# Unit 0's query tiles moved between the wide value tiles, and head pair 1 made from seven half products

## The chip, the core and the metric

The kernel runs on one core of one Trainium2 chip. The time is the device time of one execution in microseconds; several executions are taken, and their median counts. The engines are TensorE (PE, matmuls into PSUM), VectorE (DVE), ScalarE (ACT), GpSimd (POOL) and SyncE (SP, which issues most DMAs). Each runs its own list of instructions in order and waits on semaphores.

## The reference

Four layers on x of 16 x 64 rows of width 512, each added to x. The change lies in the first, an attention over a context of the same shape. Cut to that layer:

```
d, h, kv_h, g = 128, 32, 8, 4
q = rope((layernorm(x) @ Wq).reshape(b, t, 32, 128))
k = rope((ctx @ Wk).reshape(b, t, 8, 128))
v = (ctx @ Wv).reshape(b, t, 8, 128)
logits = 30 * tanh(q . k * 0.0884 / 30), masked
attn = softmax(logits) . v
x = x + attn.reshape(b, t, 4096) @ Wo
```

Behind it come a small mixture of low-rank experts, a second attention with 16 heads of 96, and a dense layer with 16 low-rank updates.

## The kernel before

All matmuls of width 512 are in float32 made from two parts: every operand is split into a high part (a copy by ACT) and a low part (the difference, by DVE or POOL), and a product takes three matmuls (high-high, high-low, low-high). A query or key tile is 128 x 512: one head's 128 columns for half of the 1024 rows, four chunks of the depth by three matmuls, twelve matmuls.

The first attention is worked through in 16 units. Unit u takes the four heads of one key head (u // 2) for one half of the rows (u % 2). Its stages: queries in four tiles, rope on them, `b0` (queries times keys, a burst of 16 short matmuls in banks 2 and 3), tanh and exp on ACT, the mask on POOL (L1271), `sum0` on DVE (transposes, a sum, a reciprocal, L1716 to L1729), a trip of the reciprocals through memory and back (`sum0_out` on SP), `norm0` (L1733), `d0` (weights times values), and `e0` (times Wo, four tiles of twelve matmuls, added to x in `e0_add`, L1547).

The queries of key head 0 (units 0 and 1) are tiles `q0(u, n)`, each with its rope. Those of the later heads come from "pairs": pair u gives two heads for all rows, and is worked in while unit u runs; it serves unit u + 2 or u + 3. A pair can be made in two ways. Plain: four tiles `pp(u, t)`, 12 matmuls each, 48 in all. By half products: seven products `p(u, k)` of 6 matmuls, 42 in all, after the manner of fast matrix multiplication by sums of blocks. That takes sums of blocks of x (made once, `xt`, split by `xt_split` into Th on ACT and Tl on DVE or POOL, L1658 and L1227), sums of blocks of the pair's weights (four 128x256 pieces on POOL, `add_weights`, L1190 to L1195, split by `pair` in one 1024 wide piece, L1220), three copies of partial results (`snap`, ACT) and three additions (`cmb`, DVE, L1618). Which pairs are plain is set by one constant, `PLAIN = 2`: pairs 0 and 1.

A rope is three DVE instructions (L1695, L1696, L1698), which read the PSUM tile and so free its bank, and one addition on POOL (L1250). A weight split is one copy on ACT (L1328) and one difference on POOL (L1213), from a ring of four staging buffers that SP fills three splits ahead.

The order is written by hand in `plan()`: a list of steps, and every engine's program goes through the same list and takes its part of each step. So a step's place in the list sets its place in the queue of each engine that has a part in it. `stage` gives a tile a PSUM bank from a ring and the step. Ahead of unit 0 stand the key tiles `k0`, the value tiles `v0`, and eight wide value tiles `vq(n)` of twelve matmuls, each copied out by ACT and sent to memory. vq, the pair of weights WS0 and the halves Th and Tl share places in memory, so that split wp(1, n) and xt_split wait for the last vq tile. The lines below have the numbers that the profile shows.

## Time and profile before

| what | value |
|---|---|
| runs | 816.91, 817.16, 817.37 us |
| median | 817.16 us |
| the profiled execution | 817.04 us, its span 815.2 us |
| busy in the span | PE 808.3, DVE 605.9, POOL 440.0, ACT 393.9 us |
| PE idle in 150 to 200 us | 1.92 us |
| PE idle in 250 to 300 us | 0 us |

The span runs from the first to the last instruction that the profiler saw. Times in the rows are microseconds from the span's start. A matmul's shown length includes its way through the array, so that the next may start before it ends; the distance of the starts is what it costs. A long length of a DVE or POOL instruction can hold a wait inside it.

### The profile page before, as it was taken

The numbers are of one execution on the slowest core, as the hardware profiler recorded it, in microseconds if no ns is written. First come the engines' busy times: TensorE is split into PE (matmuls) and PEld (weight loads), VectorE is DVE, ScalarE is ACT, GpSimd is POOL, SyncE is SP. The second block draws the span as 40 slices with busy tenths as digits, with TensorE's granted clock in tenths as the row PEclk, the third lists the DMA queues.
The fourth block names the chain that finished last, engine by engine and source line by source line (L and its number), as shares of the span: only waits on it lengthen the run. The fifth ranks groups of instructions, "written<-read, shape, count | busy, mean of one in ns | idle before, by whom it ended". The sixth has DMA issues, their size and how long they took to land.

```text
span 815.2 us, 12015 instructions
## 1 busy us (share of the span) xinstructions
PE 808.3 (99%) x4278; PEld 670.1 (82%) x4278; DVE 605.9 (74%) x1143; ACT 393.9 (48%) x960; POOL 440.0 (54%) x342
## 2 busy tenths in 40 slices
PE   9999999999999999999999999999999999999998
PEld 8898877777787777887777788899888888888887
DVE  6887579998888978888798566464466657678894
ACT  4233313334234343233433342667787777787762
POOL 4797389866767786676874520112232531365442
PEclk9999999999999999999999999999999999999999
DMA  9468402322232232322214730001110210300002
GB/s 345 157 185 339 143 14 69 100 66 72 86 117 67 77 104 77 119 78 66 77 54 126 256 105 1 27 27 52 27 27 27 66 27 14 129 15 1 1 1 104
DMA packets 34476, 70.16 MB, mean 86 GB/s; under 512 B 5360, under 2 KB 8688, under 8 KB 33776
## 3 DMA queue, kind: packets, MB, share of 16 engines
q1 hardware_dynamic: 31872, 64.54, 25.3%
q10 hardware_dynamic: 2544, 4.85, 1.7%
q8 instruction: 34, 0.56, 0.3%
q14 instruction: 26, 0.21, 0.1%
HBM read 57.70 MB, written 11.67 MB: 85 GB/s over the span
## 4 chain that ended last, share of the span: by engine, by line
PE 74%; POOL 2%; issue 1%; DVE 0%; ACT 0%; DMA 0%; ACTq 0%; POOLq 0%
PE PB L1855 14%; PE PB L1857 14%; PE PB L1856 14%; PE PB L1902 11%; PE PB L2117 8%; PE PB L2132 4%; PE PB L1862 3%; PE PB L2044 3%; PE PB L2027 2%; PE PB L2065 1%; PE PB L2079 0%; POOL W L1213 0%; DMA stage<-in_wo 0%; POOL WVl L1213 0%; POOL WSl L1213 0%
## 5 line engine op out<-in xcount | busy, mean ns | idle before, releaser
L1250 POOL TENSOR_TENSOR qb<-qb,arena 128x512 f32<-128x512 f32 x76 | 105.6, 1395 | 109.5 <-DVE arena L1698 109.5
L1328 ACT ACTIVATE Oh<-PB 96x128 fp32r<-96x128 f32 (+2 forms) x236 | 79.2, 359 | 44.6 <-PE PB L2044 25.5
L1547 DVE TENSOR_TENSOR xs<-xs,PB 128x512 f32<-128x512 f32 x111 | 73.2, 682 | 36.9 <-PE PB L1857 28.0
L1213 POOL TENSOR_TENSOR WVl<-stage,WVh 128x512 fp32r<-128x512 f32 (+1 forms) x25 | 33.6, 1359 | 70.8 <-ACT WVh L1328 64.3
L1855 PE MATMUL PB<-WVh,Oh 128*128 128x512 f32 x158 | 62.2, 394 | 0.7 <-DVE arena L1698 0.4
L1856 PE MATMUL PB<-WVl,Oh 128*128 128x512 f32 x158 | 61.5, 389 | 0.0
L1857 PE MATMUL PB<-WVh,Ol 128*128 128x512 f32 x158 | 61.5, 389 | 0.0
L1328 ACT ACTIVATE WSh<-wsum 128x1024 fp32r<-128x1024 f32 x12 | 12.7, 1061 | 91.6 <-POOL wsum L1195 91.6
L1855 PE MATMUL PB<-W,Oh 128*128 128x512 f32 x142 | 55.6, 391 | 0.8 <-POOL W L1213 0.8
L1213 POOL TENSOR_TENSOR WQl<-stage,WQh 128x512 fp32r<-128x512 f32 x17 | 22.7, 1343 | 61.0 <-ACT WQh L1328 52.2
L1857 PE MATMUL PB<-W,Ol 128*128 128x512 f32 x142 | 55.3, 389 | 0.0
L1856 PE MATMUL PB<-W,Oh 128*128 128x512 f32 x142 | 55.3, 389 | 0.0
L1695 DVE TENSOR_TENSOR qb<-PB,ropeq 128x512 f32<-128x512 f32 x64 | 44.0, 688 | 15.1 <-PE PB L1977 6.4
L1824 DVE TENSOR_TENSOR Ol<-PB,Oh 64x128 fp32r<-64x128 f32 (+2 forms) x172 | 49.2, 286 | 7.0 <-ACT Oh L1328 3.5
L1741 DVE TENSOR_TENSOR Ol<-PB,Oh 128x512 fp32r<-128x512 f32 x64 | 39.7, 682 | 18.7 <-ACT Oh L1328 18.6
L1510 ACT ACTIVATE Eb<-PB,sm 128x128 f32<-128x128 f32 x128 | 45.2, 366 | 8.9 <-DVE sm L1803 8.5
L1696 DVE TENSOR_TENSOR arena<-PB,ropeq 64x512 f32<-64x512 f32 x64 | 44.3, 693 | 0.8
L1803 DVE TENSOR_REDUCE sm<-PB 128x4 f32<-128x512 f32 x32 | 21.9, 685 | 30.7 <-PE PB L2132 30.7
L1698 DVE TENSOR_TENSOR arena<-PB,ropeq 64x512 f32<-64x512 f32 x64 | 43.7, 683 | 0.8
L2117 PE MATMUL PB<-xTh,WQh 128*128 128x512 f32 x96 | 39.8, 414 | 0.0
L2117 PE MATMUL PB<-xTh,WQl 128*128 128x512 f32 x96 | 37.7, 392 | 0.0
L2117 PE MATMUL PB<-xTl,WQh 128*128 128x512 f32 x96 | 37.6, 392 | 0.0
(343 smaller groups left out, 2457.2 us busy)
## 6 DMA issues: line engine op xcount, KB each, us to landing
stage<-in_wq SPq DMA_DIRECT2D x44, 256.0 KB, 2.8
stage<-in_wo SPq DMA_DIRECT2D x44, 256.0 KB, 2.8
arena<-recs SPq DMA_DIRECT2D x32, 256.0 KB, 3.9
stage<-in_wk SPq DMA_DIRECT2D x12, 256.0 KB, 3.8
keys<-qb SPq DMA_DIRECT2D x12, 256.0 KB, 3.2
arena<-keys SPq DMA_DIRECT2D x6, 512.0 KB, 3.3
xs<-in_x SPq DMA_DIRECT2D x8, 256.0 KB, 7.0
xf<-in_xT SPq DMA_DIRECT2D x4, 512.0 KB, 10.8
```

The lines of the kernel that those rows point to most:

```text
L1213: e.tensor_tensor(lo, src, hi.bitcast(f32), ALU.subtract).then_inc(s_wlo)
L1250: e.tensor_tensor(dst, dst, tmp, ALU.add).then_inc(s_radd)
L1328: return e.activation(dst, src, ACT.Copy)
L1510: last = e.activation(Eb[:, e2, cols], PS[:, cols], ACT.Exp, bias=mx[:, bb:bb + 1], accum_out=rs[:, bb:bb + 1])
L1547: e.tensor_tensor(xs[:, i, :], xs[:, i, :], PB[b][:, :], ALU.add).then_inc(free[b])
L1696: e.tensor_tensor(tmp[0:64], src[64:128], table[64:128, 1:2, :].broadcast_to([64, 8, 64]), ALU.mult)
L1824: last = e.tensor_tensor(dl, PA[bank_of("d1", t, bank)][d0:d0 + rows, h], dh.bitcast(f32), ALU.subtract)
L1855: e.matmul(dst, Ah, Bh, start=(k == 0), stop=False)
L1856: e.matmul(dst, Ah, Bl, start=False, stop=False)
L1857: return e.matmul(dst, Al, Bh, start=False, stop=(k == n - 1))
L1902: last = e.matmul(PB[b][:, :], W[:, w], X[:, c, :], start=fresh and c == n == 0, stop=(c == 1 and n == 2), skip_group_check=not fresh)
L2117: last = e.matmul(PB[b][:, :], W[:, m, r], H[:, c, cols], start=(n % 12 == 0), stop=(n % 12 == 11))
```

## The change

`PLAIN` becomes 1, so pair 1 is made by half products, and its products are spread over the list, with the plain tiles pp(0, 2) and pp(0, 3) between them. The tiles q0(0, 0) to q0(0, 3) stand between vq(3) and vq(7) instead of behind them. The four xt_splits come in the order (0,0), (1,0), (0,1), (1,1), of which only (1,0) has its low part on POOL, where two had it. The four splits of wo0 for units 0 and 1 stand in units 0 and 1 one by one. The steps of unit 2 get the order of the later units.

```
@@ -8,7 +8,7 @@
 NU = 16
 N1 = 32
 LO, HI = range(0, 4), range(4, 8)
-PLAIN = 2
+PLAIN = 1
 D0_BANKS = (0, 1, 4, 6)
 SLOTS = (4, 5, 6, 7, 0, 1, 2, 3)
 PARTS = {1: (0, 256), 2: (256, 512), 4: (512, 768), 5: (768, 1024), 6: (1024, 1280), 7: (1280, 1536), 3: (1536, 1792)}
@@ -303,16 +303,17 @@
     for n in range(3, 8):
         vq(n)
         spill_v(n - 1)
+        if n < 7:
+            q0(0, n - 3)
+        if n == 5:
+            step("sums", 1)
     spill_v(7)
-    q0(0, 0)
-    step("xt_split", 0, 0)
-    for n in range(1, 4):
-        q0(0, n)
     ring.remove(2)
     pair(1)
-    for n in (1, 0):
-        q0(1, n)
-    step("xt_split", 0, 1)
+    step("xt_split", 0, 0)
+    split("wo0", 0)
+    q0(1, 0)
+    step("xt_split", 1, 0)
 
     def products(u, *ks):
         for k in ks:
@@ -340,36 +341,42 @@
 
         if u == 0:
             burst(0)
+            q0(1, 1)
+            split("wo0", 1)
+            step("xt_split", 0, 1)
             q0(1, 3)
-            q0(1, 2)
-            q0p(0, 0, 5)
             step("sum0", 0)
             step("sum0_out", 0)
-            step("xt_split", 1, 0)
-            step("sums", 2)
-            q0p(0, 1, 7)
+            split("wo0", 2)
+            q0(1, 2)
+            step("xt_split", 1, 1)
+            q0p(0, 0, 6)
+            q0p(0, 1, 4)
+            norm0(0)
             continue
         if u == 1:
+            products(1, 1, 2)
             burst(1)
-            step("xt_split", 1, 1)
-            q0p(0, 2, 0)
-            q0p(0, 3, 4)
+            products(1, 5)
+            rope_p(1, 0)
+            q0p(0, 2, 1)
+            split("wo0", 3)
+            products(1, 6, 3)
+            rope_p(1, 1)
+            products(1, 7)
+            rope_p(1, 2)
+            q0p(0, 3, 3)
             for n in range(2):
                 split("wp", 2, n)
-            q0p(1, 0, 6)
-            norm0(0)
+            products(1, 4)
+            rope_p(1, 3)
+            step("sum0", 1)
+            step("sum0_out", 1)
             step("k_in", 2)
-            q0p(1, 1, 1)
             step("pair", 2)
-            q0p(1, 2, 2)
-            q0p(1, 3, 3)
-            for n in range(4):
-                split("wo0", n)
             continue
         quad = u + 2 < NU
         paired = u < NU - 3
-        if u == 2:
-            products(2, 1, 2)
         if u == NU - 2:
             step("ctx_in", 0)
         burst(u)
@@ -377,27 +384,19 @@
             step("k_in", (u + 3) // 2)
         if u in (5, 9):
             step("v_in", (u - 5) // 4)
-        if u == 2:
-            step("sum0", 1)
-            step("sum0_out", 1)
-        if u >= 4:
-            norm0(u - 1)
+        norm0(u - 1)
         if u == NU - 2:
             for m in range(3):
                 split("wk1", m, 0)
             for c in range(2):
                 split("wv1", c)
         if quad:
-            if u >= 3:
-                products(u, 1, 2)
+            products(u, 1, 2)
             products(u, 5)
             rope_p(u, 0)
-        if u == 3:
-            norm0(2)
-        if u >= 3:
-            step("sum0", u)
-            if u < NU - 1:
-                step("sum0_out", u)
+        step("sum0", u)
+        if u < NU - 1:
+            step("sum0_out", u)
         outputs(0)
         if quad:
             products(u, 6, 3)
@@ -413,19 +412,13 @@
         if u == NU - 2:
             step("ctx_in", 1)
         added(0, 1)
-        if u == 2:
-            norm0(1)
-            added(2)
         if quad:
             products(u, 4)
             rope_p(u, 3)
         if paired:
             step("pair", u + 1)
-        if u == 2:
-            step("sum0", u)
-            step("sum0_out", u)
         outputs(3)
-        added(*((3,) if u == 2 else (2, 3)))
+        added(2, 3)
         if u % 2:
             for n in range(4):
                 split("wo0", 2 * u - 2 + n)
@@ -1042,7 +1035,7 @@
                 return (("k0", 6, 1), ("vq", 7))[k[0]] if k[0] < 2 else ("p", k[0] - 2, 4) if k[0] >= 2 + PLAIN else ("pp", k[0] - 2, 3)
             if kind == "wo0":
                 h = k[0] - 4
-                return ("e0", h // 4 * 2 + 1, 3) if h >= 0 else ("q0", 1, 3)
+                return ("e0", h // 4 * 2 + 1, 3) if h >= 0 else (("vq", 7), ("q0", 1, 0), ("q0", 1, 1), ("q0", 1, 2))[k[0]]
             if kind == "wk1":
                 return {(0, 0): ("p", 13, 4), (1, 0): ("p", 13, 4), (2, 0): ("p", 13, 4), (0, 1): ("k1", 0, 0, 1),
                         (1, 1): ("k1", 0, 1, 1), (2, 1): ("k1", 1, 1, 1)}[k]
@@ -1220,10 +1213,9 @@
                     e.tensor_tensor(lo[:, 768:1792], wsum[:, :], hi[:, 768:1792].bitcast(f32), ALU.subtract).then_inc(s_wslo)
                 elif kind == "xt_split":
                     kk, hf = k
-                    if (kk + hf) % 2:
-                        n = 2 * kk + hf
+                    if (kk, hf) == (1, 0):
                         hi, lo, src = (H[:, 2 * kk:2 * kk + 2, 512 * hf:512 * hf + 512] for H in (Th, Tl, xf))
-                        pool.wait_ge(s_thi, n + 1)
+                        pool.wait_ge(s_thi, 2)
                         e.tensor_tensor(lo, src, hi.bitcast(f32), ALU.subtract).then_inc(s_tlo[1])
                 elif kind == "many":
                     pool.wait_ge(s_tab, 16)
@@ -1441,8 +1433,8 @@
                         if u:
                             act.wait_ge(*done("e0", u - 1, 3))
                         else:
-                            act.wait_ge(s_tlo[0], 2)
-                            act.wait_ge(s_tlo[1], 2)
+                            act.wait_ge(s_tlo[0], 3)
+                            act.wait_ge(s_tlo[1], 1)
                         move(dh, src).then_inc(s_ohi)
                 elif kind == "ffn_xT":
                     i, = k
@@ -1652,9 +1644,9 @@
                     e.tensor_tensor(b[1, 1], b[1, 1], b[0, 1], ALU.subtract).then_inc(s_xt)
                 elif kind == "xt_split":
                     kk, hf = k
-                    if (kk + hf) % 2 == 0:
+                    if (kk, hf) != (1, 0):
                         hi, lo, src = (H[:, 2 * kk:2 * kk + 2, 512 * hf:512 * hf + 512] for H in (Th, Tl, xf))
-                        dve.wait_ge(s_thi, 2 * kk + hf + 1)
+                        dve.wait_ge(s_thi, 2 * hf + kk + 1)
                         e.tensor_tensor(lo, src, hi.bitcast(f32), ALU.subtract).then_inc(s_tlo[0])
                 elif kind == "rope":
                     n = ropes[tuple(k)]
@@ -1886,7 +1878,7 @@
                     pe.wait_ge(*(lo_ready("wp", u, t // 4) if t in (1, 2, 4) else (s_wslo, u - PLAIN + 1)))
                     pe.wait_ge(*x_ready(1))
                     if t in (4, 5, 6, 7):
-                        pe.wait_ge(s_tlo[t in (6, 7)], 1 + (t in (4, 7)))
+                        pe.wait_ge(s_tlo[t == 7], {5: 1, 6: 2, 4: 3, 7: 1}[t])
                     if t == 6:
                         pe.wait_ge(s_snap, 3 * (u - PLAIN) + 1)
                     elif t == 3:
```

Where instructions stand on the engines shows in three places. On DVE, behind the reciprocal of unit 0's sum0: the names are tiles, PB0 to PB7 the PSUM banks, Tl the low part of x's block sums. Before, the bank of the plain tile pp(0,1) is roped there, then xt_split(1,1), then the plain tiles of unit 1's stretch:

```order
L1729 RECIPROCAL rec<-rec 64x32
L1695 TENSOR_TENSOR qb<-PB7,ropeq 128x8x64
L1696 TENSOR_TENSOR arena<-PB7,ropeq 64x512
L1698 TENSOR_TENSOR arena<-PB7,ropeq 64x512
L1658 TENSOR_TENSOR Tl<-xf,Th 128x2x512
L1695 TENSOR_TENSOR qb<-PB0,ropeq 128x8x64
L1696 TENSOR_TENSOR arena<-PB0,ropeq 64x512
L1698 TENSOR_TENSOR arena<-PB0,ropeq 64x512
L1695 TENSOR_TENSOR qb<-PB4,ropeq 128x8x64
```

Now q0(1,2) is roped there, then xt_split(1,1), and then the two first plain tiles of pair 0, and then comes norm0(0):

```order
L1721 RECIPROCAL rec<-rec 64x32
L1687 TENSOR_TENSOR qb<-PB1,ropeq 128x8x64
L1688 TENSOR_TENSOR arena<-PB1,ropeq 64x512
L1690 TENSOR_TENSOR arena<-PB1,ropeq 64x512
L1650 TENSOR_TENSOR Tl<-xf,Th 128x2x512
L1687 TENSOR_TENSOR qb<-PB6,ropeq 128x8x64
L1688 TENSOR_TENSOR arena<-PB6,ropeq 64x512
L1690 TENSOR_TENSOR arena<-PB6,ropeq 64x512
L1687 TENSOR_TENSOR qb<-PB4,ropeq 128x8x64
L1688 TENSOR_TENSOR arena<-PB4,ropeq 64x512
L1690 TENSOR_TENSOR arena<-PB4,ropeq 64x512
L1725 TENSOR_TENSOR Eb<-Eb,arena 128x1024
```

What moved: sum0(0) stands two ropes earlier than before, so that both plain tiles come behind it and behind the xt_split; the first cmb of pair 1 follows norm0(0). On POOL, in the stretch of unit 1, before, from the rope addition that follows the wsum pieces of pair 2:

```order
L1250 TENSOR_TENSOR qb<-qb,arena 128x8x64
L1271 TENSOR_TENSOR pTb<-pTb,keep 128x1024
L1250 TENSOR_TENSOR qb<-qb,arena 128x8x64 x2
L1213 TENSOR_TENSOR WSl<-stage,WSh 128x512
L1213 TENSOR_TENSOR WSl<-stage,WSh 128x256
L1250 TENSOR_TENSOR qb<-qb,arena 128x8x64 x2
L1220 TENSOR_TENSOR WSl<-wsum,WSh 128x1024
L1250 TENSOR_TENSOR qb<-qb,arena 128x8x64 x2
L1213 TENSOR_TENSOR WVl<-stage,WVh 128x512 x2
L1213 TENSOR_TENSOR W<-stage,W 128x512 x2
```

Now the wsum pieces of pair 2 stand behind the rope additions of unit 1, directly ahead of the split of wp(2,0) (WSl, 512 wide):

```order
L1242 TENSOR_TENSOR qb<-qb,arena 128x8x64 x2
L1206 TENSOR_TENSOR W<-stage,W 128x512
L1242 TENSOR_TENSOR qb<-qb,arena 128x8x64 x3
L1183 TENSOR_TENSOR wsum<-stage 128x256
L1184 TENSOR_TENSOR wsum<-stage 128x256
L1186 TENSOR_TENSOR wsum<-wsum,stage 128x256
L1188 TENSOR_TENSOR wsum<-stage,wsum 128x256
L1206 TENSOR_TENSOR WSl<-stage,WSh 128x512
L1206 TENSOR_TENSOR WSl<-stage,WSh 128x256
L1242 TENSOR_TENSOR qb<-qb,arena 128x8x64
```

What moved: the splits of pair 2 and its sums stand behind all rope additions but one, and the split of wo0 stands between these. On PE, ahead of the burst b0 of unit 2, before, the last two matmuls of p(2,2) and then d0(0):

```order
L1902 MATMUL PB7<-xTl,WSh1 128x512
L1902 MATMUL PB7<-xTh,WSl1 128x512
L2044 MATMUL PB0<-Eb,arena 128x256
L2044 MATMUL PB1<-Eb,arena 128x256
L2044 MATMUL PB0<-Eb,arena 128x256
L2044 MATMUL PB1<-Eb,arena 128x256
L2044 MATMUL PB4<-Eb,arena 128x256
L2044 MATMUL PB6<-Eb,arena 128x256
L2044 MATMUL PB4<-Eb,arena 128x256
L2044 MATMUL PB6<-Eb,arena 128x256
```

Now d0(0) ends and b0(2) is followed by p(2,1), whose weights are WSh1 and WSl1:

```order
L2036 MATMUL PB4<-Eb,arena 128x256
L2036 MATMUL PB6<-Eb,arena 128x256
L2019 MATMUL PB2<-qb,arena 64x256 x4
L2019 MATMUL PB3<-qb,arena 64x256 x4
L1894 MATMUL PB5<-xTh,WSh1 128x512
L1894 MATMUL PB5<-xTl,WSh1 128x512
L1894 MATMUL PB5<-xTh,WSl1 128x512
L1894 MATMUL PB5<-xTh,WSh1 128x512
```

What moved: p(2,1) and p(2,2), which stood ahead of d0(0), stand behind b0(2).

## Rows read from the trace of the kernel before

**Rows 1.** The page: its head and the busy times (share, instructions).
```profile
span 815.2 us, 12015 instructions
...
PE 808.3 (99%) x4278; PEld 670.1 (82%) x4278; DVE 605.9 (74%) x1143; ACT 393.9 (48%) x960; POOL 440.0 (54%) x342
```
**Rows 2.** Windows: length, busy time of each engine, granted clock, DMA share, GB/s.
```profile
150.00:200.00 50.00, 48.08 (x236) 36.80 (x235) 44.92 (x69) 15.41 (x26) 33.20 (x28) 1.00 0.31 85
...
250.00:300.00 50.00, 50.00 (x251) 39.58 (x250) 43.48 (x68) 19.18 (x35) 36.38 (x30) 1.00 0.26 75
```
**Rows 3.** Waits of PE: who for whom, us in total, times, longest.
```profile
PE PB L1902 <- DVE xs L1547: 1.3, 1, 1.3
...
PE PB L1855 <- POOL W L1213: 0.8, 3, 0.3
...
PE PB L1855 <- DVE arena L1698: 0.4, 1, 0.4
```
**Rows 4.** Timeline of PE: start, length, engine, line, instruction.
```profile
95.75 0.39 PE L1972 MATMUL PB<-xTh,WVh 128*128 128x512 f32 x1
...
111.84 0.39 PE L1857 MATMUL PB<-xTh,WVl 128*128 128x512 f32 x1
...
114.03 0.50 PE L1855 MATMUL PB<-xTh,WR 128*128 128x512 f32 x1
...
168.52 2.00 PE L2044 MATMUL PB<-pTb,arena 64*128 64x256 f32 x16
```
**Rows 5.** Timeline of PE at its longest break.
```profile
175.32 0.51 PE L1902 MATMUL PB<-xTh,WSh 128*128 128x512 f32 x1 [1.33 <-DVE xs L1547]
```
**Rows 6.** Timeline of DVE.
```profile
98.67 0.69 DVE L1695 TENSOR_TENSOR qb<-PB,ropeq 128x512 f32<-128x512 f32 x1 [6.41 <-PE PB L1977]
...
100.79 1.23 DVE L1658 TENSOR_TENSOR Tl<-xf,Th 128x1024 fp32r<-128x1024 f32 x1
...
139.41 1.33 DVE L1733 TENSOR_TENSOR Eb<-Eb,arena 128x1024 f32<-128x1024 f32 x1
...
153.93 2.38 DVE L1727 TENSOR_TENSOR rec<-pair 64x32 f32<-64x32 f32 x1
...
170.62 1.25 DVE L1716 STREAM_TRANSPOSE arena<-Eb 128x1024 f32<-128x1024 f32 x1
...
174.65 0.62 DVE L1547 TENSOR_TENSOR xs<-xs,PB 128x512 f32<-128x512 f32 x1
...
180.86 2.03 DVE L1733 TENSOR_TENSOR Eb<-Eb,arena 128x1024 f32<-128x1024 f32 x1 [0.41 <-DMA arena<-recs]
```
**Rows 7.** Timeline of POOL.
```profile
100.84 2.33 POOL L1250 TENSOR_TENSOR qb<-qb,arena 128x512 f32<-128x512 f32 x1 [13.44 <-DVE arena L1698]
...
110.25 2.54 POOL L1213 TENSOR_TENSOR WSl<-stage,WSh 128x512 fp32r<-128x512 f32 x2
...
128.34 0.75 POOL L1190 TENSOR_TENSOR wsum<-stage 128x256 f32<-128x256 f32 x1
...
130.56 0.74 POOL L1195 TENSOR_TENSOR wsum<-stage,wsum 128x256 f32<-128x256 f32 x1
...
153.88 2.38 POOL L1271 TENSOR_TENSOR Eb<-Eb,keep 128x1024 f32<-128x1024 f32 x1
```
**Rows 8.** Timeline of ACT.
```profile
96.44 1.05 ACT L1328 ACTIVATE Th<-xf 128x1024 fp32r<-128x1024 f32 x1
97.39 1.14 ACT L1328 ACTIVATE WSh<-stage 128x512 fp32r<-128x512 f32 x2
98.43 1.05 ACT L1328 ACTIVATE Th<-xf 128x1024 fp32r<-128x1024 f32 x1
```
**Rows 9.** Timeline of PE at the program's start.
```profile
0.97 4.64 PE L1939 MATMUL PB<-pTb 128*128 128x128 f32 x20 [0.97 <-POOL psum L1253]
6.04 0.77 PE L1929 MATMUL PB<-cTh,WKh 128*128 128x512 f32 x1 [0.43 <-ACT cTh L1328]
6.61 0.57 PE L1932 MATMUL PB<-cTh,WKl 128*128 128x512 f32 x1
```

## The prediction

> **What bounds the kernel now.** I read the page first: TensorE (PE) is busy 808.3 of a span of 815.2 us [rows 1]. The windows show where the rest goes: PE idles 1.92 us in 150 to 200 us, and nothing in 250 to 300 us, where the half products already run in the order that the change spreads to head pair 1 [rows 2]. The list of waits has five breaks on PE's matmuls of this part, the largest of 1.3 us [rows 3]. So each matmul taken out counts in full if nobody makes PE wait, and I have to ask who could. VectorE (DVE) works 44.9 of 50 us just behind the changed place and GpSimd (POOL) 33.2 [rows 2]; the change moves DVE's work against PE's, so the whole question is whether DVE stays ahead.
>
> **Matmuls.** From the first matmul of q0(0,0) at 95.75 us to the last of the sixth tile at 111.84 us there are 71 steps: 0.2266 us each, 2.72 us for a tile of twelve, 1.36 us for a half product of six [rows 4]. Pair 1 needed four tiles, 48 matmuls, and now seven half products, 42: 6 x 0.2266 = **1.36 us less**.
>
> **Breaks that go.** At 175.32 us PE waits for DVE's add into xs: unit 2 has its sum0 and norm0 in an unusual place, so DVE is late there [rows 5]. The starts lie 1.72 us apart, 1.50 over the step, 0.17 more than the idle shown. The five breaks, all from 150 to 210 us, are 1.3 + 0.8 + 0.4 = 2.5 us idle [rows 3]; with 0.17 for each, **3.4 us**. In the new order unit 2 is like the later units, which have none; I take all of it as gone.
>
> **Prices for the rest.** A rope (three DVE instructions) takes 2.12 us, from 98.67 to 100.79 us, and an xt_split on DVE 1.2 us [rows 6]. DVE's sum0 takes 4.03 us, from 170.62 to 174.65 us; norm0 1.3 us; a cmb is one 128x512 instruction, 0.7 us like each third of a rope [rows 6]. On POOL a 128x512 piece takes 1.27 us and a 1024 wide one 2.4 us; the four wsum pieces take from 128.34 to 131.30 us, 2.96 us [rows 7]. On ScalarE (ACT) a 1024 wide copy takes 0.95 us until the next starts and 1.05 us to its end, two splits 1.04 us [rows 8]. A burst b0 takes 2.19 - 0.23 = 1.96 us between tiles, d0 2.0 us [rows 4]. I carry 0.1 us for PE's slower restart.
>
> **One more price: DVE and POOL exclude each other** when DVE's instruction has both inputs in SBUF. At 100.84 us POOL's 1.27 us piece, begun just behind DVE's xt_split of 100.79 us, took 2.33 us; at 153.93 us DVE's 64x32 add, begun just behind POOL's 2.38 us piece, took 2.38 us [rows 6, 7]. Ropes, which read PSUM, are not held. The GPSIMD Engine Reference of the Trainium skill (Specifications) says the same in general: the two share their SBUF interfaces, with contention when a DVE instruction has two SBUF inputs. By that rule, the trace agrees. Were it not so, the walk below would lose its first wait and the sum would be about 819.3 us.
>
> **The walk, on the clock of the trace before.** Four q0 tiles now come before the last vq tiles: vq(7) ends at 95.75 + 4 x 2.72 = 106.64 us. PE without waits: q0(1,0) to 109.4, b0(0) to 111.3, q0(1,1), q0(1,3), q0(1,2), pp(0,0), pp(0,1) to 125.0, p(1,1), p(1,2) to 127.8, then b0(1). DVE must meanwhile do 3 xt_splits, 4 ropes of unit 1, sum0(0), two ropes of pair 0, norm0(0), 3 cmb and three more ropes before p(1,4) may start: 3.6 + 8.5 + 4.0 + 4.2 + 1.3 + 2.1 + 6.4 = 30.1 us, and PE's own way from q0(1,0)'s end to p(1,4) is 120 matmuls and two bursts, 27.2 + 3.9 = 31.1 us. There is 1 us of room, and DVE starts late:
> ACT copies vq(7), splits wp(1,0) and wp(1,1), copies the pair, and gives Th(0,0) at about 110.2 us. POOL began the 1024 wide low part of the pair at 109.9 us, so DVE gets in at 112.1 and is through at 113.3 us instead of starting a rope at 109.6. Ropes of q0(1,0) and q0(1,1) to 117.5; POOL then holds the next xt_split until 118.9 (its own Th(1,0) piece), 120.1; rope q0(1,3) 122.2; POOL's mask, held behind DVE, ends at 122.5; sum0(0) 126.5; rope q0(1,2) 128.6. The xt_split that follows holds POOL's add exactly as in the row of 100.84 us, 2.4 us behind the rope's end: 131.0 us. b0(1) needs that add and was ready at 127.8: **wait 3.2 us**, with all of PE queued behind it.
> DVE goes on: xt_split 129.8, ropes 131.9 and 134.0, norm0(0) 135.3, cmb 136.0, ropes of p(1,0) 138.1 and pp(0,2) 140.3, cmb 141.0, rope 143.1, cmb 143.8. PE after b0(1) at 131.0 reaches p(1,4) at 144.0: no wait, by 0.2 us. Then p(1,4) 145.4, d0(0) 147.5, b0(2) 149.5, whose rope add is there at 147.3.
> Now p(2,1) stands behind the burst; before, it stood ahead of it and its weights had been split earlier. Its low part comes from POOL, in whose queue it stands behind the rope add of pp(0,3): DVE ropes to 145.9 and 148.1, POOL's add 149.3, the four wsum pieces 152.3, the split 153.5: **wait 4.0 us**. Then wp(2,1) 0.7, a rope add 1.27 and the pair's 2.4 us give the sums at 157.9; p(2,1) and p(2,2) end at 156.4: **wait 1.5 us** at p(2,5).
> norm0(1) comes 10.2 us behind the start of sum0(1), as from 170.62 to 180.86 us [rows 6], at 160.4; with cmb, rope, sum0(2), cmb, rope, cmb DVE is at 172.1, PE at p(2,4) at 171.6, and e0(0,3) then waits for bank 7: **0.5 and 0.7 us**. Later units stand as before.
>
> **Sum.** The profiled execution before took 817.04 us, its span 815.2; the median of the runs is 817.16. 817.04 - 1.36 - 3.4 + 3.2 + 4.0 + 1.5 + 1.2 = 822.2, and four new restarts at 0.1 make 822.6; the 0.12 us between that execution and the median is lost in the rounding. A difference under 0.2% (1.6 us) can't be told from none.
>
> **Costs at nothing.** The three snaps and the wider pair copy on ACT hide: ACT works 15.4 of 50 us [rows 2]. The q0 ropes of unit 0 now run while DVE has no vq work. wo0's splits leave the end of unit 1, where they stood right ahead of e0(0,0), but each goes in front of rope adds, 1.27 us of POOL; uncovered they would lengthen the first wait by up to 1.27 us. Loads on SP stand behind sum0_out(0) until the reciprocal at 126.5 us; wp(2,1) is wanted at 150, so 20 us cover it.
>
> **The rivals.**
> **DVE keeps up (faster).** If DVE's rope of q0(1,2) ends by 124.3 us and POOL splits wp(2,0) by 149.5, no new wait stays: 817.04 - 1.36 - 3.4 = 812.3. For it speaks only that unit 4 and later do with this order [rows 2]; against it, the room of 1 us against an xt_split that alone starts 2.6 us late. 0.08.
> **POOL's second chain is covered.** Without the 4.0 and 1.5 us and their restarts: 816.9, no change to tell. It would need DVE's rope of pp(0,3) 4 us earlier, against the count of DVE's work. 0.07.
> **POOL goes first more often.** DVE and POOL come within 0.1 us of each other at the xt_split of 128.6 and at norm0(0) of 134.0. If POOL wins both, DVE is 2.3 us later at the cmb ahead of p(1,4), and everything behind it with it: 824.9. The row of 100.79 shows DVE winning such a start, the row of 153.93 POOL with an earlier one [rows 6, 7]. 0.17.
> **The clock falls in a wait.** The first full-width matmuls are 0.57 us apart, against 0.2266 once PE has been at work [rows 9]: 1.2 instead of 2.4 GHz. From PE's first matmul at 0.97 us to the end of that step at 7.2 us is some 6 us, 10 such steps instead of 26, so a like stretch would cost 16 x 0.2266 = 3.6 us. After the first wait DVE's next lateness hides much of it; after the 4 us wait nothing does: 826.2. The longest break of the trace behind its start is the 1.33 us, and the granted clock stays full in its stretch [rows 2], so the trace does not decide it. 0.10.
> TensorE: Matmul & The Clock Gate of the Trainium skill (What's actually happening) says that throttled is the default and that idling brings it back; no run here shows yet whether waits of this size do.
> **The forecast**, DVE late by about 3 us at b0(1) and POOL's split late by about 4 us at p(2,1), 821.0 to 824.0: 0.55. The last 0.03 lies beyond either end.
>
> **Range.** The low end reaches halfway into the first two rivals, 819.5, which leaves out their 0.15; the high end takes in the last, 826.2. Faster by over 0.2% 0.08, within 0.2% 0.07, slower 0.85.
>
> **What would show it.** PE's waits: one at the second b0 burst of about 3 us ended by POOL's rope add; one of about 4 us at L1894, the first product behind the third burst, ended by POOL's WSl split; one of 1.5 us six to twelve matmuls on, ended by POOL's WSl from wsum; the wait of 1.3 us on xs gone. DVE's first xt_split should take about 2 us more than 1.23. From 250 us on, every burst should come later by one constant. Wrong would be: no wait at the second burst, or more than 5 us of waits behind the fourth burst, or a matmul step of over 0.3 us behind a wait.

## The result, and the profile after

The changed kernel takes 824.61 us (median of 4, 822.08 to 824.77) against 817.26 us before: ratio 1.0081, 95% interval 1.0067 to 1.0094. It is slower by 7.35 us; the forecast was 822.6, within 819.5 to 826.2. Its profiled execution took 824.62 us, its span 822.8. One of the five executions of e1 below took 2892.31 us, most of its 512 wide matmuls 0.84 us apart at a granted clock that reads 1.00, and one of the 19 of the kernel before that stand beside e5 to e8 took 1636.61 us: both are in the medians given (e1's is 822.31 us without) and in none of the ratios.

The page of the changed kernel, its head and busy times (they answer to [rows 1]):

```profile
span 822.8 us, 12021 instructions
...
PE 808.4 (98%) x4272; PEld 670.5 (81%) x4272; DVE 607.8 (74%) x1147; ACT 395.7 (48%) x964; POOL 442.1 (54%) x346
```

PE has six matmuls less and is busy for as long as before: something made the others longer. The windows of the changed kernel (they answer to [rows 2]; the number behind POOL's is the granted clock):

```profile
100.00:150.00 50.00, 46.86 (x222) 36.20 (x222) 39.95 (x54) 15.82 (x24) 38.61 (x26) 0.97 0.21 59
150.00:200.00 50.00, 44.28 (x207) 34.39 (x205) 41.89 (x68) 15.44 (x26) 30.89 (x27) 0.97 0.26 72
200.00:250.00 50.00, 50.00 (x251) 39.61 (x250) 42.17 (x67) 17.52 (x30) 36.23 (x30) 1.00 0.33 98
250.00:300.00 50.00, 50.00 (x251) 39.61 (x250) 42.28 (x66) 18.46 (x31) 36.31 (x30) 1.00 0.27 75
```

All idle time of these four windows lies between 100 and 200 us, and there the granted clock is 0.97. Waits of PE, whole run (they answer to [rows 3]):

```profile
PE PB L1894 <- POOL WSl L1206: 4.1, 1, 4.1
PE PB L2019 <- POOL qb L1242: 3.1, 1, 3.1
PE PB L1921 <- ACT cTh L1320: 1.6, 1, 1.6
PE PB L1894 <- DVE PB L1610: 1.2, 1, 1.2
...
PE PB L1847 <- DVE arena L1690: 0.4, 1, 0.4
```

The two large waits are at the places that were forecast, with the forecast releasers. Timeline of PE around them:

```profile
110.30 1.95 PE L2019 MATMUL PB<-qb,arena 128*64 128x256 f32 x16
...
131.93 3.42 PE L2019 MATMUL PB<-qb,arena 128*64 128x256 f32 x16 [3.14 <-POOL qb L1242]
135.28 0.66 PE L1894 MATMUL PB<-Th,WSh 128*128 128x512 f32 x1
...
155.81 0.49 PE L1894 MATMUL PB<-xTh,WSh 128*128 128x512 f32 x1 [4.06 <-POOL WSl L1206]
...
158.24 0.63 PE L1894 MATMUL PB<-xTh,WSh 128*128 128x512 f32 x1
158.66 0.63 PE L1894 MATMUL PB<-xTl,WSh 128*128 128x512 f32 x1
...
175.24 0.47 PE L1894 MATMUL PB<-Th,WSh 128*128 128x512 f32 x1 [1.25 <-DVE PB L1610]
...
177.28 0.50 PE L1847 MATMUL PB<-WVh,Oh 128*128 128x512 f32 x1 [0.41 <-DVE arena L1690]
...
182.38 1.95 PE L2019 MATMUL PB<-qb,arena 128*64 128x256 f32 x16
```

The same burst of 16 matmuls takes 1.95 us at 110.30 and 3.42 us behind the first wait; behind the second the steps are 0.43 us instead of 0.2266. That is the 1.2 GHz level instead of 2.4. Timeline of DVE, and the two pieces of POOL at the first two of its rows:

```profile
111.04 3.25 DVE L1650 TENSOR_TENSOR Tl<-xf,Th 128x1024 fp32r<-128x1024 f32 x1 [3.97 <-ACT Th L1320]
...
118.45 2.66 DVE L1650 TENSOR_TENSOR Tl<-xf,Th 128x1024 fp32r<-128x1024 f32 x1
...
152.39 1.25 DVE L1708 STREAM_TRANSPOSE arena<-pTb 128x1024 f32<-128x1024 f32 x1
...
163.68 1.22 DVE L1725 TENSOR_TENSOR pTb<-pTb,arena 128x1024 f32<-128x1024 f32 x1 [4.56 <-DMA arena<-recs]
```

```profile
110.83 2.38 POOL L1213 TENSOR_TENSOR WSl<-wsum,WSh 128x1024 fp32r<-128x1024 f32 x1
...
117.63 2.40 POOL L1219 TENSOR_TENSOR Tl<-xf,Th 128x1024 fp32r<-128x1024 f32 x1
```

Two xt_splits take 3.25 and 2.66 us instead of 1.23 [rows 6]: each began while POOL was in a piece of 2.4 us, and ended 1.1 us behind that piece's end. The last row of DVE is norm0(1): DVE stands idle 4.56 us until the reciprocals of sum0(1) are back, with cmb and rope queued behind it.

### The profile page after: what moved, and what is told of

Its sections match the earlier page's. It is cut to its first block, busy times and chain, and to the rows that moved or that the text cites. A ratio compares the mean times of both kernels' runs of the same rounds, so it can differ in the third digit from the quotient of the medians.

```text
span 822.8 us, 12021 instructions
## 1 busy us (share of the span) xinstructions
PE 808.4 (98%) x4272; PEld 670.5 (81%) x4272; DVE 607.8 (74%) x1147; ACT 395.7 (48%) x964; POOL 442.1 (54%) x346
## 4 chain that ended last, share of the span: by engine, by line
PE 78%; DVE 1%; issue 0%; ACT 0%; ACTq 0%; DVEq 0%
PE PB L1847 14%; PE PB L1849 14%; PE PB L1848 14%; PE PB L1894 13%; PE PB L2109 8%; PE PB L2124 3%; PE PB L2036 3%; PE PB L1854 3%; PE PB L2019 3%; PE PB L2057 1%; PE PB L2071 0%; DVE arena L1690 0%; DVE arena L1688 0%; DVE Ol L1733 0%; DVE PB L1610 0%
## 5 line engine op out<-in xcount | busy, mean ns | idle before, releaser
L1894 PE MATMUL PB<-Th,WSh 128*128 128x512 f32 x104 | 40.8, 392 | 1.2 <-DVE PB L1610 1.2
L1894 PE MATMUL PB<-Th,WSl 128*128 128x512 f32 x104 | 40.5, 389 | 0.0
L1894 PE MATMUL PB<-Tl,WSh 128*128 128x512 f32 x104 | 40.5, 389 | 0.0
## 6 DMA issues: line engine op xcount, KB each, us to landing
xf<-in_xT SPq DMA_DIRECT2D x4, 512.0 KB, 10.2
```

The lines of the kernel that those rows point to most:

```text
L1894: last = e.matmul(PB[b][:, :], W[:, w], X[:, c, :], start=fresh and c == n == 0, stop=(c == 1 and n == 2), skip_group_check=not fresh)
```

## The experiments

All ratios are to the kernel before, timed beside it on the same chip; its medians there were 817.16 to 817.62 us. Where two profiles are compared, I take the start of a burst b0 and subtract the difference at b0(0), since the program's first 60 us vary between executions (below). In the expectations theory A is that DVE is late over the whole stretch, so that what one wait hides the next one shows; theories B and C are that the wait in question has a cause of its own.

### e1 and e5: work for PE in the two waits

```
+ if u == 1:                      # ahead of b0(1)'s wait on the rope additions
+     13 matmuls of xTh with xTh into bank 2
+ if (u, t) == (2, 1):            # ahead of p(2,1)'s wait on the split
+     17 matmuls of xTh with xTh into bank 5
```

> The changed kernel, with 13 extra 512-wide matmuls (2.95 us) into b0(1)'s own bank ahead of its wait of 3.14 us, and 17 (3.85 us) into p(2,1)'s bank ahead of its wait of 4.06 us; their results are overwritten, so the output is unchanged. TensorE then has work in both waits. Clock theory: the burst that took 3.35 us behind the first wait takes 1.95 us, and the nine steps of 0.43 us behind the second take 0.2266 us; since the wait at p(2,5) that I had forecast then comes back (about 1.2 us), the total falls by about 1.5 to 2 us, to 822.6 to 823.1. If all of the slow stretch were on the path: 3.4 us less, 821.2. If the slow burst has another cause (operands from POOL just written): no change, 824.6, and the 3.35 us burst stays.

> The same kernel as e1_fill (13 and 17 extra matmuls in the two waits), once more, because that one's profiled execution was a disturbed one. Its other executions took 821.9 to 823.3 us. Clock theory: here the burst b0(1) behind the first wait takes 1.95 us instead of 3.4, no stretch behind either wait has steps of 0.43 us, the granted clock of the whole run is 1.00, and the total is again 822 to 823 us. Else: the 3.4 us burst stays.

Measured: 822.74 us (ratio 1.0064, 1.0050 to 1.0077) and 822.39 us (1.0061, 1.0044 to 1.0077). Timeline of PE in e5_fill_again:

```profile
127.60 3.11 PE L1859 MATMUL PB<-xTh 128*128 128x512 f32 x13
130.93 1.95 PE L2028 MATMUL PB<-qb,arena 128*64 128x256 f32 x16 [0.22 <-POOL qb L1242]
132.81 0.50 PE L1900 MATMUL PB<-Th,WSh 128*128 128x512 f32 x1
...
149.81 4.19 PE L1859 MATMUL PB<-xTh 128*128 128x512 f32 x17 [0.66 <-DVE arena L1690]
...
157.58 0.47 PE L1900 MATMUL PB<-Th,WSh 128*128 128x512 f32 x1 [0.87 <-POOL WSl L1213]
```

The burst is back at 1.95 us and no slow step is left; the run's clock is 1.00. PE did nothing useful more, and the kernel is about 2 us faster. The other executions say the same: all seven others of e1 and e5 that count have a granted clock of 1.000, the four of the changed kernel 0.995 to 0.998. And a wait appears that the changed kernel did not show: 0.87 us at p(2,5), where I had forecast 1.5. At the slow clock PE had come too late to meet it. So the fall of the clock is shown as a cost of its own. Taking it away brings b0(5) forward by 1.6 us (2.67 us earlier than in the changed kernel, of which 1.03 is there at b0(0)); that is less than PE loses in the slow stretches (3.3 us, below), since PE then comes early enough to wait for the others.

### e2: the sums of pair 2 early

```
+ step("sums", 2)              # between products 6, 3 and product 7
  products(1, 7)
  rope_p(1, 2)
- q0p(0, 3, 3)
+ stage("pp", 0, 3, bank=3)
  for n in range(2):
      split("wp", 2, n)
+ rope_p(0, 3)
```

> The changed kernel with POOL's four wsum pieces of pair 2 between the products 6,3 and 7 of pair 1 instead of directly ahead of the split of wp(2,0), and both splits of wp(2,n) ahead of the rope of pp(0,3). Theory A (VectorE is the late engine of this whole stretch, and what one wait hides the next shows): the 4.06 us wait at p(2,1) falls below 0.5 us, b0(2) waits 1 to 1.5 us for POOL's rope addition, and VectorE, whose queue is no earlier, makes PE wait some 3 us at p(2,5) for bank 0 and some 3 to 4 us at p(2,4) for its cmb: 824 to 827 us. Theory B (the split's late place is a fault by itself): its 4.1 us and the slow clock's 1.6 us come back, 818.9 us.

Measured: 825.61 us, ratio 1.0101 (1.0084 to 1.0117). Waits of PE in its first 300 us:

```profile
PE PB L2021 <- POOL qb L1244: 4.2, 2, 3.1
PE PB L1896 <- DVE Ol L1735: 2.5, 1, 2.5
PE PB L1896 <- DVE PB L1612: 1.6, 1, 1.6
```

The 4.1 us wait for the split is gone, and nothing is won: 1.1 us more at b0(2) (the 4.2 are 3.1 and 1.06), 2.5 us at p(2,5) for bank 0, 0.4 more at p(2,4). The wait named POOL; what it stood for was DVE, whose queue no edit to POOL's list had made earlier. Theory B falls.

### e3: q0(1,2) ahead of sum0(0)

```
  q0(1, 3)
+ q0(1, 2)
  step("sum0", 0)
  step("sum0_out", 0)
  split("wo0", 2)
- q0(1, 2)
```

> The changed kernel with q0(1,2), its rope and its rope addition ahead of sum0(0) instead of behind it, which is what b0(1)'s wait of 3.14 us is for. Theory A: that wait falls under 0.5 us, but sum0(0) ends 2.1 us later, its reciprocals come back about 6 us behind it, and norm0(0) holds VectorE's queue: PE waits 5 to 6 us at p(1,4) for cmb instead, 825 to 828 us. Theory B: the wait of 3.1 us and the 1.5 us of slow clock behind it come back, 820.0 us.

Measured: 826.95 us, ratio 1.0116 (1.0100 to 1.0131). Waits of PE, first 300 us, and DVE's norm0(0):

```profile
PE PB L1894 <- DVE PB L1610: 8.6, 2, 7.5
PE PB L1894 <- POOL WSl L1206: 1.7, 1, 1.7
```

```profile
138.22 2.90 DVE L1725 TENSOR_TENSOR Eb<-Eb,arena 128x1024 f32<-128x1024 f32 x1 [1.90 <-DMA arena<-recs]
```

The first wait is gone, and 7.5 us stand at p(1,4): norm0(0) now waits 1.9 us for its reciprocals and is then held by POOL besides (2.90 instead of 1.23 us). I had forecast 5 to 6. Behind the 7.5 us the clock is down too: from p(1,4) to b0(2) PE takes 6.07 us instead of 3.38.

### e4: xt_split(0,0) ahead of POOL's 1024 wide piece

```
- pair(1)
+ for n in range(2):
+     split("wp", 1, n)
  step("xt_split", 0, 0)
+ step("pair", 1)
```

> The changed kernel with xt_split(0,0) ahead of the 1024 wide split of pair 1, so that VectorE's instruction starts before POOL's 2.38 us piece instead of behind it (there it took 3.25 us, 2.0 more than 1.23). Exclusion theory: the xt_split takes about 1.25 us, ends near 110.5 us and the first rope of q0(1,0) starts as soon as its tile is there. But VectorE then waits for PE's next tile, so only 1.0 to 1.3 of the 2 to 3 us reach b0(1): its wait 2 us instead of 3.1, total 823.4. If all came through: 822 or less. If the 3.25 us were the instruction's own waiting for ACT, nothing changes: 824.6.

Measured: 822.49 us, ratio 1.0063 (1.0050 to 1.0075). Timelines of DVE and of POOL:

```profile
110.13 1.22 DVE L1652 TENSOR_TENSOR Tl<-xf,Th 128x1024 fp32r<-128x1024 f32 x1 [3.03 <-ACT Th L1322]
...
115.27 0.69 DVE L1689 TENSOR_TENSOR qb<-PB,ropeq 128x512 f32<-128x512 f32 x1 [1.91 <-PE PB L1851]
```

```profile
108.92 3.03 POOL L1208 TENSOR_TENSOR WSl<-stage,WSh 128x512 fp32r<-128x512 f32 x2 [0.45 <-ACT WSh L1322]
```

DVE's instruction is back at 1.22 us and it is POOL's two pieces that take 3.03 instead of 1.98 us. That is the exclusion, seen from both sides. Of the 2.9 us that DVE gained, 1.91 went into waiting for q0(1,1); b0(1) waited 2.26 us instead of 3.14, and b0(5) came 0.94 us earlier. The medians lie 2.1 us apart; the profiles bear 0.9 of it out.

### e6: pair 1 plain in the new order

```
- PLAIN = 1                    + PLAIN = 2
- step("sums", 1)              + step("sums", 2)    # the latter ahead of split wp(2, 0)
- step("pair", 1)              # no 1024 wide piece on ACT and POOL
- products(1, 1, 2)            + q0p(1, 0, 5)
- products(1, 5) ... (1, 6, 3) + q0p(1, 1, 7)
- products(1, 7)               + q0p(1, 2, 0)
- products(1, 4)               + q0p(1, 3, 5)
```

> The changed kernel with pair 1 plain again (four tiles of twelve matmuls, no cmb, no snap), everything else of the change kept: the q0 tiles between the vq tiles, the order of xt_split, the splits of wo0, unit 2 in the later units' order. Theory A (the balance of VectorE against PE decides: three cmb, 2.1 us, less for it and 1.36 us more for PE in the same stretch): waits of about 2 us stay at b0(1) and at p(2,1) and 1.8 us at p(2,5), none at the last tile of pair 1: 819 to 821 us. Theory B (the half products are a gain, only the new order costs): 824.6 + 1.4 = 826.0 us.

Measured: 819.67 us, ratio 1.0024 (1.0015 to 1.0034). Waits of PE, first 300 us:

```profile
PE PB L1888 <- POOL WSl L1200: 1.9, 1, 1.9
PE PB L2013 <- POOL qb L1236: 1.4, 1, 1.4
```

Six matmuls more, and 4.9 us less. Timeline of DVE:

```profile
111.84 2.24 DVE L1644 TENSOR_TENSOR Tl<-xf,Th 128x1024 fp32r<-128x1024 f32 x1 [3.24 <-ACT Th L1314]
```

b0(1) waits 1.40 us and its burst stays fast, the split is waited for 1.91 us instead of 4.06. The expectation puts this down to three cmb less in DVE's queue, but ahead of b0(1) no cmb of pair 1 has run in either kernel. What is gone there is pair 1's 1024 wide piece on ACT and POOL: xt_split(0,0) is waited for 3.24 us instead of 3.97 and takes 2.24 us instead of 3.25, and sum0(0) starts 11.36 us behind b0(0)'s start instead of 13.11. These 1.75 us are the difference of the two waits (3.14 and 1.40 us). How much of the later gain is the cmb's the run does not separate. The half products of pair 1 save 1.36 us of PE and cost about 6 elsewhere, and the clock has a part in these 6: seven of the nine executions of e6 have a granted clock of 1.000. The profiled one, 821.67 us, was its slowest.

### e7: the q0 tiles back behind vq(7)

```
- if n < 7:
-     q0(0, n - 3)             # inside the vq loop, step("sums", 1) with it
  ...
+ q0(0, 0)
+ step("xt_split", 0, 0)       # was behind pair(1)
+ step("sums", 1)
+ for n in range(1, 4):
+     q0(0, n)
```

> The changed kernel with q0(0,0) to q0(0,3) behind the last vq tile again, xt_split(0,0) behind the first of them as before the change. VectorE then no longer stands idle for 4 us ahead of xt_split(0,0) (3.97 us in the changed kernel), but it gets its first query tile 5 us later. Theory A: the two nearly cancel; b0(0) waits 1.5 us for the rope of q0(0,3), b0(1) 3 us or a little less, total 825 to 826 us. Theory C (the idle time ahead of xt_split is what makes VectorE late): the first wait falls by its 4 us, 821 us.

Measured: 824.41 us, ratio 1.0078 (1.0065 to 1.0091), the same as the changed kernel. b0(0) waited 1.42 us and b0(1) 2.49. The idle 3.97 us of DVE ahead of xt_split(0,0) were the price of its earlier start, not the reason of its lateness; theory C falls, and theory A's total was 1 us too high.

### e8: unit 2's order alone, in the kernel before

```
- if u == 2:
-     step("sum0", 1) ...      # behind b0(2)
+ step("sum0", 1) ...          # at unit 1's end
- if u == 2:
-     norm0(1); added(2)       # behind added(0, 1)
+ norm0(u - 1) from u = 3 on, norm0(1) behind rope_p(2, 0)
- if u == 2: sum0(2)           # behind pair 3
+ sum0(2)                      # behind norm0(1)
```

> The kernel before with only unit 2's steps in the order of the later units (sum0 and norm0 of unit 1 ahead, added(2) back), which I had credited with the whole 3.4 us of breaks. Forecast's term: 817.2 - 3.4 = 813.8 us. Theory A (unit 2's unusual order was there because VectorE is late at that point): the wait of 1.3 us on xs goes and a wait of about 3 us for bank 0 at p(2,5) comes, and one of 1.5 us at p(2,4): 817 to 819 us.

Measured: 818.88 us, ratio 1.0012 (1.0003 to 1.0021). Waits of PE, first 300 us:

```profile
PE PB L1895 <- DVE Ol L1734: 2.9, 1, 2.9
...
PE PB L1895 <- DVE PB L1611: 0.5, 1, 0.5
```

The wait of 1.3 us on xs and the three for W are gone, and 2.9 us at p(2,5) stand in their place (3 were expected, and 1.5 at p(2,4), where 0.49 came). The odd order of unit 2 was what let PE pass there. It is not quite the changed kernel's order: p(2,1) and p(2,2) stay ahead of b0(2), and norm0(1) stands behind a rope.

### e9: DVE's work made shorter

```
+ w = 1 if k[0:2] in (["q0", 1], ["p", 0], ["p", 1]) else 8
- e.tensor_tensor(tmp[0:64], src[64:128], ...)
+ e.tensor_tensor(tmp[0:64, 0:w], src[64:128, 0:w], ...)    # the other half alike
```

> The changed kernel with VectorE's second and third rope instruction only 64 instead of 512 columns wide for q0(1,n), pp(0,t) and p(1,t): twelve ropes, each some 1.2 us shorter, so the arena keeps old values and the queries of those heads are not those of the reference; order, waits and all of PE, ACT and POOL stay. Theory A (VectorE is late in this stretch because of the sum of its work): about 5 us come back; the wait at b0(1) falls from 3.1 to 2.2 us (sum0(0) then waits for POOL's mask, so no more), that at p(2,1) from 4.1 to about 1.7 us, p(2,5) waits 1.7 us, that at p(2,4) halves: 817 to 819.5 us. Theory B (each wait has a local cause in POOL's queue: the mask and wsum pieces): both waits stay within 0.5 us, 824 us.

Measured: 818.16 us, ratio 1.0005 (0.9997 to 1.0014). Waits of PE, first 300 us:

```profile
PE PB L1895 <- POOL WSl L1206: 1.6, 1, 1.6
PE PB L1895 <- POOL WSl L1213: 1.3, 1, 1.3
PE PB L2020 <- POOL qb L1242: 1.3, 1, 1.3
...
PE PB L1895 <- DVE PB L1610: 1.0, 1, 1.0
```

The order on every engine and all semaphores are those of the changed kernel; the queries of these heads are wrong. 6.4 of its 7.35 us are gone, the fall of the clock with them (1.00). The wait at b0(1) is 1.25 us where 2.2 were expected, that at p(2,1) 1.62 where 1.7 were. So both waits that name POOL were mainly DVE's; 5.5 us in smaller ones are left (1.25, 1.62, 1.28, 0.96 and 0.43).

### e10: two plain pairs, other engines' steps moved

The order of the steps, as a difference to the kernel before (its core; PE's own order is not touched). The places were picked by replaying the queues with the durations of the trace of before.

```
 q0(1,3) q0(1,2) pp(0,0)
-rope p(0,0)   sum0(0)   sum0_out(0)   xt_split(1,0)   sums(2)
+sum0(0)   sums(2)   rope p(0,0)                  # xt_split(1,0) ahead of b0(0)
 ...
+split wp(2,0)
 pp(0,3)
+norm0(0)
 rope p(0,3)
-split wp(2,0)
 ...
-rope p(1,3)   split wo0 0   split wo0 1 ...
+split wo0 1   split wo0 2   split wo0 3   rope p(1,3)
 p(2,1) p(2,2) d0(0,0) 
+cmb(2,2)
 d0(0,1)
+sum0(1)
 b0(2)
-sum0(1)
 ...
 p(2,4)
-rope p(2,3)   pair 3   sum0(2)
+pair 3   sum0(2)   rope p(2,3)
```

> The kernel before (two plain pairs, 48 matmuls for pair 1) with nothing changed but the places of VectorE's, POOL's and ACT's steps in units 0 to 2: sum0(0) ahead of the rope of pp(0,0); norm0(0) ahead of the rope of pp(0,3); sum0(1) ahead of b0(2) and the cmb of p(2,2) between the halves of d0(0); the split of wp(2,0) one tile earlier; the splits of wo0 spread; the ropes of p(1,2), p(1,3), p(2,2), p(2,3) later; all xt_splits but the last ahead of unit 0. PE's own order is the same. If the five breaks of before are VectorE's and POOL's order alone, PE keeps one of 1.2 us at 172 us and the small ones at 203 us: 817.2 - 3 = 814.2 us. If they move elsewhere: 817 us.

Measured: 814.74 us, ratio 0.9968 (0.9959 to 0.9978): faster than both kernels. Windows, and waits of PE in the first 300 us:

```profile
150.00:200.00 50.00, 49.16 (x248) 38.65 (x245) 45.93 (x75) 18.55 (x32) 36.79 (x29) 1.00 0.29 80
```

```profile
PE PB L1908 <- DVE arena L1704: 0.8, 1, 0.8
PE PB L1935 <- ACT cTh L1334: 0.7, 2, 0.4
PE PB L1861 <- POOL W L1219: 0.3, 1, 0.3
```

DVE works 45.93 of 50 us, more than in either kernel, and PE waits less: the same work in another order.

### e11: half products, other engines' steps moved

```
 vq(7)
-split wp(1,0)  split wp(1,1)  pair 1  xt_split(0,0)  split wo0 0
+pair 1  xt_split(0,0)  split wp(1,0)  split wp(1,1)
 q0(1,0)
-rope q0(1,0)  xt_split(1,0)  b0(0)
+b0(0)  xt_split(1,0)  rope q0(1,0)
 ...
 q0(1,3)
+sum0(0)
 rope q0(1,3)
-sum0(0)
 ...                            # splits of wo0 later
-xt_split(1,1)
 pp(0,0)  rope p(0,0)  pp(0,1)
+xt_split(1,1)
 ...
-rope p(1,2)  pp(0,3)  rope p(0,3)  split wp(2,0)
+pp(0,3)  rope p(1,2)  split wp(2,0)
 p(1,4)
+pair 2  rope p(0,3)  split wp(2,1)
 ...
 p(2,5)  rope p(2,0)
+norm0(1)                      # was behind b0(2)
```

> The changed kernel, PE's tiles in its order (but pp(0,3) as there, b0(0) as there) and pair 1 by half products, with the other engines' steps moved: the 1024 wide split of pair 1 behind the first xt_split, sum0(0) ahead of the rope of q0(1,3), the splits of wo0 later, xt_split(1,1) behind the rope of pp(0,0), norm0(1) behind the rope of p(2,0), the ropes of p(1,2) and pp(0,3) later, the split of wp(2,0) ahead of p(1,4). Theory A' (the lateness is in the order of the queues as much as in the sum of work): the wait at b0(1) goes, 1.4 us stay at p(1,4), 2.2 at p(2,1), 0.9 at p(2,5): 817 to 819 us, level with before at best. If the sum of VectorE's work alone decides: 822 us or more.

The expectation has one place wrong: in the kernel as run, pair 1's 1024 wide piece stands ahead of the first xt_split on ACT and POOL, not behind it (POOL's begins at 108.62 us, and the xt_split that starts at 109.52 takes 2.57 us).

Measured: 819.55 us, ratio 1.0025 (1.0017 to 1.0034); no wait is over 2.14 us and the clock is 1.00. b0(1) still waits 0.82 us, p(1,4) 1.00, p(2,1) 2.14, p(2,5) 1.50. Order alone takes 5 us off the changed kernel, 0.55 us less than the forecast's 819 would need, and the half products still end behind before.

### e12: norm0(1) behind the rope of p(2,0)

```
- norm0(u - 1)                 # behind b0(u)
+ if u > 2: norm0(u - 1)
  products(u, 5)
  rope_p(u, 0)
+ if u == 2: norm0(1)
```

> The changed kernel with norm0(1) behind the cmb and the rope of p(2,0) instead of directly behind b0(2). In the changed kernel VectorE stood idle for 4.56 us ahead of norm0(1), for the reciprocals' way through memory, with a cmb and a rope queued behind it. If that idle time is what makes the cmb ahead of p(2,4) late: the wait of 1.25 us at p(2,4) goes, one of about 0.3 us stays for bank 7, and the total falls by 1.5 us to 823.1. If p(2,4)'s wait has another cause: no change, 824.6. The two large waits, 3.1 and 4.1 us, stay in both cases.

Measured: 821.85 us, ratio 1.0063 (1.0049 to 1.0076). Waits of PE, first 300 us, and DVE's norm0(1):

```profile
PE PB L1897 <- POOL WSl L1209: 4.1, 1, 4.1
PE PB L2022 <- POOL qb L1245: 3.2, 1, 3.2
```

```profile
162.19 1.23 DVE L1728 TENSOR_TENSOR pTb<-pTb,arena 128x1024 f32<-128x1024 f32 x1
```

Cmb and rope now fill the time of the reciprocals' way, norm0(1) starts without a wait, 0.7 us earlier (1.49 less the 0.76 that b0(0) was earlier), and both breaks at p(2,4) and e0(0,3) are gone. By b0(5) it is 2.7 us (3.47 less 0.76), where I had expected 1.5. The clock fell behind both large waits as before.

## Why the prediction was right, point by point

The sign, the range and the two large waits came as forecast. The time lies 2.0 us above the 822.6, and above the 821.0 to 824.0 that had 0.55. That it is not further off is luck in part: by the profile the clock's 3.3 us, 0.9 us of a later start and 0.9 more at the last two waits were missing in the sum, and 1.6 of a third wait that did not come and 1.5 by which the breaks were taken too small stood against them. And one of the prediction's own signs of being wrong came: matmul steps of over 0.3 us behind a wait.

**What bounds the kernel.** Right. The whole question was whether DVE keeps ahead: with DVE's ropes cut (e9) the loss all but goes, with POOL's list mended (e2) it stays.

**Matmuls, 1.36 us.** Right by count; from 231.28 us on every burst comes 7.53 us later than before (b0(5) at 223.75 before), up to b0(14), 443.65 and 451.18.

**Breaks that go, 3.4 us.** Gone (but for 0.41 us for DVE's rope, which now stand one unit earlier, at e0(0,3)); the term was too small and bore its price elsewhere. From b0(3) to b0(5) the kernel before took 53.30 us (170.45 to 223.75), the changed one 48.90: 4.4 us, and 0.45 more at 153.98 us, 4.9 in all. I had counted the idle time and 0.17 for each; another 0.1 goes with the second step behind each break, 0.45 lie in two d0 (from 195.46 and 221.60 us it is 2.16 and 2.15 us to the next burst instead of 1.93), and 0.4 in slower steps at 190.2 and 218.3 us for which no wait is listed. As a gain of unit 2's order by itself the term was false: e8, nearly that order alone, costs 1 us.

**The exclusion of DVE and POOL.** Right: 3.25 us where 3.2 were worked out, and e4 shows both directions. The GPSIMD Engine Reference of the Trainium skill (Specifications) says that VectorE and GpSimd share their SBUF interfaces, with contention when a VectorE instruction has two SBUF inputs; by that rule, the traces agree.

**First wait, 3.2 us at b0(1).** 3.14 us, by POOL's rope addition. **Second wait, 4.0 us at p(2,1).** 4.06 us, by POOL's WSl split. Both of the size and the releaser forecast; that their common source is DVE is what e2 and e9 add. What made DVE late at the first is in part POOL's 1024 wide piece of pair 1 (e4, e6).

**Third wait, 1.5 us at p(2,5).** Not there, because of the clock (below); 0.87 us in e5.

**POOL goes first more often, a rival at 0.17.** Did not come, though its 824.9 lies near the measured time: the xt_split at 129.53 us and norm0(0) at 134.92 us took 1.23 us each, and POOL's two additions behind them 2.30 and 2.34. DVE won both starts. **DVE keeps up** and **POOL's second chain is covered** fell with the two waits.

**The clock, in no term of the sum, a rival at 0.10.** This was the step that failed. I wrote that behind the first wait DVE's lateness would hide the fall and that the trace of before does not decide it behind the second. It fell behind both. The first burst took 1.47 us more, and the step behind it 0.50 instead of the 0.34 behind b0(0): 1.63 us. Behind the second, from p(2,1) to p(2,4) are 72 matmuls in 19.43 us, of which 1.41 are a wait and 16.3 work: 1.7 us. The rival had one fall at 3.6 us, worked out from the 0.57 us steps of the program's start; it was two at about 1.7 with steps of 0.43. That the two together come near its 3.6 us is chance.

**0.5 us at p(2,4), 0.7 at e0(0,3).** 1.25 and 0.41 us idle. The step that was off is "norm0(1) comes 10.2 us behind the start of sum0(1)": it was 11.3 us (152.39 to 163.68). e12 shows that this idle time of DVE was on the path, with more than its waits.

**The sum by the runs,** b0(5) to b0(5), each wait with its restart: 0.86 at the start - 1.36 - 4.9 + 3.21 + 1.63 + 4.13 + 1.70 + 1.52 + 0.69 = 7.48 us, against 7.53 measured. The 0.86 us is no part of the change: the common part of the program began later in this execution, as the wait for cTh of 1.6 us against 0.43 [rows 9] shows. In the twelve profiles of the changed kernel and of e2 to e12 this start lay from 0.2 us earlier to 2.4 us later than in that of before, so that two profiles tell no part of under 1 us unless their starts are taken off.

**By parts of the change:** unit 2's order, as far as e8 has it, costs 1.0 us (its ratio; its interval goes from 0.2 to 1.7); all of the change but the half products 2.0 (e6's); the half products the other 4.9 (the medians of e6 and of the changed kernel; by the ratios 4.7 of 6.6). Of what they cost, order takes back most: e11 is 5.1 us faster than the changed kernel. But with two plain pairs the same means give more (e10, 814.74). Whether half products of pair 1 in some other order of PE's tiles could pay was not tried.

## What to carry to other kernels

A wait names the engine that released it, not the one that is late: POOL's pieces were on time for what DVE gave them. Before a step is made from less work for the bottleneck and more for its neighbour, add up the neighbour's work between two points that both must pass, including holds and the time it stands behind a DMA's way; 1 us of room was too little for 2 us of hold. And if the neighbour is late, move a step that has to wait for a DMA behind work that is ready, before taking work off: reordering alone won 2.9 us here with no matmul saved.

## What the runs showed of the hardware

**The clock falls behind short waits, and not always.** It fell behind waits of 1.91 (e6), 2.26 (e4), 2.49 (e7), 2.50 (e2), 2.90 (e8), 3.14, 3.16 (e12), 4.06 and 7.51 us (e3), and stayed up behind 1.69 (e3), 2.14 (e11) and, once, 3.14 us (e2), where the burst took 1.95 us. This timeline of e2 shows the latter, and the fall behind its 2.50 us, whose slow steps begin 1 us after the wait:

```profile
132.72 1.95 PE L2021 MATMUL PB<-qb,arena 128*64 128x256 f32 x16 [3.14 <-POOL qb L1244]
...
157.84 0.50 PE L1896 MATMUL PB<-Th,WSh 128*128 128x512 f32 x1 [2.50 <-DVE Ol L1735]
...
161.03 0.63 PE L1849 MATMUL PB<-WVh,Oh 128*128 128x512 f32 x1
```

Up to the burst of 132.72 us this program is that of the changed kernel: a wait of the same length with and without the fall. What decides it no run here shows. This may be why the executions of one kernel lie some us apart: of the changed kernel's four, the one at 822.08 us has a granted clock of 0.998, those at 824.60 to 824.77 have 0.995 or 0.996. A cost of about 1.7 us (2.7 behind the 7.51 us of e3) belongs beside every wait of about 2 us or more as a chance, not as a certainty. TensorE: Matmul & The Clock Gate of the Trainium skill (What's actually happening) says that the state depends on how busy PE has been of late; by that rule, filling the waits should keep the clock, and e5 agrees.
